# Vision transformer block on one core: the low parts of one weight row move from VectorE to GpSimd, and the layer-norm statistics start right behind the second block of low parts

## What is computed

```python
h = _L0_tok_ref(x, ln_gamma, ln_beta, W, b)     # shifted patches, layer norm over 3840 values, einsum to 192
h = concatenate([cls_tok, h], axis=1)
h = h + _L0_attn_ref(_layernorm(h), w_q, b_q, w_k, b_k, w_v, b_v, w_o, b_o, bias_table)   # 12 heads of 16
h = h + _L0_ffn_ref(_layernorm(h), router_w, w_gate, w_up, w_down, ws_gate, ws_up, ws_down, sg_w, sg_b)
return h                                        # (16, 37, 192)
```

## Time and profile before

| | |
|---|---|
| median of 3 runs | 155.25 us (154.12 to 157.67) |
| the profiled execution | 153.76 us, of which span 151.7 us |
| PE busy | 136.1 us, 90% of the span |
| DVE busy | 105.2 us, 69% |
| ACT busy | 85.6 us, 56% |
| POOL busy | 50.8 us, 33% |
| mean granted TensorE clock | 0.989 of full speed |

### The profile page before, as it was taken

How to read it: one execution, slowest core, us unless ns; L and a number is a source line. 1 busy time by engine, 2 the same in 40 slices (tenths; PEclk the granted TensorE clock), 3 DMA queues, 4 the chain that set the end, 5 groups by cost and what they waited for, 6 DMA issues and landing times.

```text
span 151.7 us, 3991 instructions
## 1 busy us (share of the span) xinstructions
PE 136.1 (90%) x1554; PEld 107.3 (71%) x1554; DVE 105.2 (69%) x268; ACT 85.6 (56%) x206; POOL 50.8 (33%) x72
## 2 busy tenths in 40 slices
PE   7769999999969879995869999998999999999991
PEld 2228678875558768975538868886887888888890
DVE  6499997899978768895275999857946423423553
ACT  0578779632687794663258877556455344444330
POOL 8038002400000000000003334388478477477330
PEclk9999999999999999998799999999999999999999
DMA  4999992095002323006993000146980000000003
GB/s 122 394 370 389 289 289 64 7 322 244 0 4 68 64 68 64 4 4 209 393 413 127 4 0 0 64 135 231 295 250 3 0 0 4 0 0 4 2 0 120
DMA packets 10580, 19.05 MB, mean 126 GB/s; under 512 B 2886, under 2 KB 6290, under 8 KB 10562
## 3 DMA queue, kind: packets, MB, share of 16 engines
q1 hardware_dynamic: 10218, 18.48, 37.2%
q10 hardware_dynamic: 344, 0.32, 0.8%
HBM read 17.84 MB, written 0.96 MB: 124 GB/s over the span
## 4 chain that ended last, share of the span: by engine, by line
PE 49%; DVE 27%; ACT 10%; issue 5%; DMA 4%; POOL 2%; DVEq 0%; SPq 0%; POOLq 0%; ACTq 0%
PE PS L810 22%; PE PS L840 12%; DVE we L1247 6%; DMA slab<-in_w_inner_dram 4%; DVE xhl L1225 2%; DVE bst L1356 2%; PE PS L622 2%; PE PS L670 2%; DVE piece L1296 2%; DVE vhl L1561 2%; PE PS L700 1%; POOL vhl L1182 1%; ACT piece L961 1%; DVE h L1390 1%; DVE xs L1440 1%
## 5 line engine op out<-in xcount | busy, mean ns | idle before, releaser
L1191 POOL TENSOR_TENSOR kq<-vhl,kq 128x296 f16<-128x296 f32 x35 | 28.2, 805 | 71.2 <-ACT kq L1098 71.1
L1561 DVE SCALAR_TENSOR_TENSOR vhl<-PS,vhl 128x296 f32<-128x296 f32 x36 | 16.8, 465 | 21.2 <-POOL vhl L1182 13.7
L1091 ACT ACTIVATE vhl<-PS 128x296 f32<-128x296 f32 x36 | 14.9, 415 | 25.3 <-PE PS L810 25.2
L1098 ACT ACTIVATE kq<-vhl 128x296 f16<-128x296 f32 x36 | 16.0, 445 | 4.2 <-DVE vhl L1561 4.2
L1182 POOL TENSOR_TENSOR vhl<-vhl,xs 128x296 f32<-128x296 f32 x14 | 12.5, 892 | 6.8 <-issue 6.1
L810 PE MATMUL PS<-XAh,piece 128*128 128x296 f16 x48 | 9.5, 289 | 1.6 <-ACT XAh L978 0.7
L810 PE MATMUL PS<-XAh,slab 128*128 128x296 f16 x48 | 10.0, 289 | 0.7 <-DVE vhl L1561 0.7
L1247 DVE SCALAR_TENSOR_TENSOR we<-slab,gbs,we 128x192 f32<-128x192 f32 x24 | 9.0, 444 | 2.0 <-ACT we L899 2.0
L810 PE MATMUL PS<-XAh,xsq 128*128 128x296 f16 x48 | 10.0, 289 | 0.0
L502 PE MATMUL PS<-whl,xhl 128*128 128x192 f16 (+1 forms) x40 | 9.9, 247 | 0.0
L504 PE MATMUL PS<-whl,xhl 128*128 128x192 f16 (+1 forms) x40 | 9.9, 246 | 0.0
(11 more groups left out here) (242 smaller groups left out, 367.3 us busy)
## 6 DMA issues: line engine op xcount, KB each, us to landing
slab<-in_w_inner_dram SPq DMA_DIRECT2D x3, 960.0 KB, 9.4
xs<-gate_rows_dram SPq DMA_DIRECT2D x8, 296.0 KB, 6.3
xs<-in_x_inner_dram SPq DMA_DIRECT2D x3, 592.0 KB, 10.3
stage<-in_f_a_dram SPq DMA_DIRECT2D x2, 768.0 KB, 4.7
stage<-in_f_b_dram SPq DMA_DIRECT2D x2, 768.0 KB, 6.3
stage<-gate_rows_dram SPq DMA_DIRECT2D x8, 148.0 KB, 6.0
stage<-in_f_d_dram SPq DMA_DIRECT2D x2, 576.0 KB, 7.2
xhl<-in_f_a_dram SPq DMA_DIRECT2D x1, 768.0 KB, 8.8
```

Source lines behind the costliest of these rows:

```text
L1091: A(silu[:, i % 2, :], PS[:, 3 + 2 * (i % 2), 0:HALF], ACT.Silu, scale=1.0 / XW).then_inc(S["a_silu"], 1)
L1098: A(ah[:, f % ABUF, half * HALF:(half + 1) * HALF], hf[:, i % 3, :], ACT.Copy).then_inc(S["a_ah"], 1)
L1191: G.tensor_tensor(al[:, f % ABUF, cols], hf[:, i % 3, :], ah[:, f % ABUF, cols], ALU.subtract).then_inc(S["g_al"], 1)
L1561: V.scalar_tensor_tensor(out=hf[:, i % 3, :], in0=PS[:, 4 + 2 * (i % 2), 0:HALF], scalar=SH / XW, in1=src[:, i % 2, :], op0=ALU.mult, op1= ...
```

## The change

Three things are changed.

1. The low parts of piece 2 (row 96 of `WC`) are made on GpSimd. It first scales the row of `awst` into a new buffer `brow` (1 x 1161), and then subtracts the high parts in four instructions (128, 128, 256 and 393 columns), each of which waits for the one before. It signals `g_br`, for which TensorE waits in the places where it waited for the last `v_awl`. VectorE loses five instructions in `queries_keys_low(2)` and one in `values_low(2)`.
2. `column_total()` stands ahead of `last_patches(2)` on TensorE.
3. VectorE waits for `csum` inside `centred(0)`, and `centred(1)` stands behind `rsqrt(0)`.

```diff
--- before.py
+++ after.py
@@ -162,6 +162,7 @@
         awst = sb("awst", [P, 3, AW])
         WAh, WAl, WB = (sb(n, [P, PW], F16) for n in ("WAh", "WAl", "WB"))
         WC = sb("WC", [CROWS, PW], F16)
+        brow = sb("brow", [CROWS, AW])
         kodd = sb("kodd", [P, 1])
         keven = sb("keven", [P, 1])
 
@@ -232,7 +233,7 @@
                    a_fw a_silu a_ah
                    v_one v_ind v_pad v_aw0 v_kk v_xl v_fold v_ring v_wl v_mr v_awl v_stat v_c v_h v_hn v_lo  v_kb v_sg v_max v_sub
                    v_cn v_rd v_lg v_dif v_gate v_gx v_fw v_hf v_acc v_fin v_al v_bn
-                   g_tab g_mk g_one g_vz g_v1 g_rows g_sg g_al""".split()
+                   g_tab g_mk g_one g_vz g_v1 g_rows g_br g_sg g_al""".split()
         S = {n: sem(n) for n in names}
 
         def bank(b, rows=P):
@@ -568,8 +569,8 @@
             for t in (0, 1):
                 last_patches(t)
             statistics()
+            column_total()
             last_patches(2)
-            column_total()
             for t in (0, 1, 2):
                 bias(t)
             for t in (3, 4):
@@ -615,7 +616,10 @@
                     pe.wait_ge(S["v_c"], TILES)
                 if f == 0 and i in (0, 2, 4):
                     pe.wait_ge(S["a_aw"], 3 + 3 * (i // 2))
+                if f == 0 and i in (0, 2):
                     pe.wait_ge(S["v_awl"], 5 + 5 * (i // 2))
+                if f == 0 and i == 4:
+                    pe.wait_ge(S["g_br"], 4)
                 c0 = ((KA, KB), (QA, QB))[q][g]
                 if f in (0, 4):
                     tokens_ready(0, half, i)
@@ -639,7 +643,8 @@
             def values(i):
 
                 pe.wait_ge(S["a_aw"], 12)
-                pe.wait_ge(S["v_awl"], 18)
+                pe.wait_ge(S["v_awl"], 12)
+                pe.wait_ge(S["g_br"], 5)
                 if i >= 2:
                     pe.wait_ge(S["a_hi"], 4)
                     pe.wait_ge(S["v_lo"], 4)
@@ -1169,6 +1174,23 @@
             G.memset(CA[:, N:NPAD], 0.0)
             G.memset(CC[:, N:NPAD], 0.0).then_inc(S["g_rows"], 1)
 
+            pool.wait_ge(S["g_rows"], 2)
+            pool.wait_ge(d_aw[2], 48)
+            G.tensor_scalar(brow[96:CROWS, :], awst[96:CROWS, 2, :], SW, None, ALU.mult).then_inc(S["g_br"], 1)
+            pool.wait_ge(S["a_aw"], 9)
+            low = slice(96, CROWS)
+            heads = brow[low, 0:VC].rearrange("p (q c) -> p q c", q=2)
+            for g in (0, 1):
+                pool.wait_ge(S["g_br"], g + 1)
+                h = heads[:, :, g * P:(g + 1) * P].rearrange("p q (r c d) -> p c q r d", r=LANES, c=2)[:, 0]
+                G.tensor_tensor(lane_cols(WC[low], g), h, lane_cols(WC[low], g), ALU.subtract).then_inc(S["g_br"], 1)
+            pool.wait_ge(S["g_br"], 3)
+            G.tensor_tensor(third_packed(WC[low, QB:VP]), heads[:, :, 2 * P:3 * P], third_packed(WC[low, QB:VP]),
+                            ALU.subtract).then_inc(S["g_br"], 1)
+            pool.wait_ge(S["g_br"], 4)
+            pool.wait_ge(S["a_aw"], 12)
+            G.tensor_tensor(WC[low, VP:PW], brow[low, VC:AW], WC[low, VP:PW], ALU.subtract).then_inc(S["g_br"], 1)
+
 
             def gated(i):
 
@@ -1264,7 +1286,7 @@
                 cols = sum_half(half)
                 V.tensor_copy(sumrows[rows, cols], PS[rows, half, 0:cols.stop - cols.start]).then_inc(S["v_mr"], 1)
 
-            low_of = ((WAl, WAh, slice(0, P)), (WB, WB, slice(64, P)), (WC, WC, slice(96, CROWS)))
+            low_of = ((WAl, WAh, slice(0, P)), (WB, WB, slice(64, P)))
 
             def queries_keys_low(k):
 
@@ -1296,7 +1318,7 @@
                 V.scalar_tensor_tensor(out=W[r0:P, part], in0=st[r0:P, part], scalar=SW, in1=hi[r0:P, part],
                                        op0=ALU.mult, op1=ALU.subtract).then_inc(S["v_fw"], 1)
 
-            for k in range(3):
+            for k in range(2):
                 queries_keys_low(k)
 
             stat = [0]
@@ -1326,6 +1348,8 @@
             nmean, nsq = small[:, 6, :], small[:, 7, :]
 
             def centred(t):
+                if t == 0:
+                    dve.wait_ge(S["a_cs"], 2)
                 dve.wait_ge(S["p_main"], (2, 2, 3, 5, 5)[t])
                 V.scalar_tensor_tensor(out=t1[:, t, :], in0=csum[:, :], scalar=small[:, 6, t:t + 1],
                                        in1=patch_out(t), op0=ALU.mult,
@@ -1339,10 +1363,9 @@
             step(V.scalar_tensor_tensor(out=small[:, 3, :], in0=sums[:, 1], scalar=1.0 / (32 * PATCH_DIM), in1=nsq,
                                         op0=ALU.mult, op1=ALU.add))
             step(V.tensor_scalar(small[:, 0, :], small[:, 3, :], 0.0, EPS, ALU.max, ALU.add))
-            dve.wait_ge(S["a_cs"], 2)
-            for t in (0, 1):
-                centred(t)
+            centred(0)
             rsqrt(0, 1.0 / (SPIX * SPW))
+            centred(1)
 
             bn = [0]
 
@@ -1415,7 +1438,6 @@
             normed(0, (3, 4))
             keys_third(1)
             values_low(1)
-            values_low(2)
             low_parts(0, (1, 2, 0), 1)
 
             def differences(u):
```

## The result

| | before | changed |
|---|---|---|
| median | 154.69 us (4 runs, 153.63 to 157.67) | 157.62 us (4 runs, 156.34 to 158.82) |
| ratio, 95% interval | | 1.027 (1.020 to 1.035) |

The change makes the kernel slower by 2.7%, and 0.5% faster was forecast. That it is slower is clear of the interval; whether by more than 2% is not. The profiled execution took 158.82 us and has a span of 156.8 us; it is the longest of the four, because the clock fell for long in it, so its span is not used for differences, only its rows.

The account below looks back on a forecast made before the run. It took 28 to 44 us as bound by VectorE's chain of small steps, not TensorE. Gain 0.89 us less hold-ups 0.15 us gives 0.74 us; 155.25 - 0.74 = 154.5 us, range 152.9 to 156.7 us.

Parts of the forecast that it names:

- What GpSimd costs VectorE: Step on VectorE's small steps, 28.4 to 34 us: hold-ups by GpSimd cost 0.15 us, between 0 and 2.0 us.
- The bound of 0.40 us for one hold-up: Worst VectorE wait seen: a `we` instruction of 805 ns, median 410 ns, begun beside a GpSimd subtraction of 0.63 us.
- the five steps: VectorE instructions reading two SBUF operands, 28.4 to 34 us: one statistics step, three in `rsqrt(0)`, one in `values_low(0)`; 0.40 us each at most.
- hold-ups eat the gain: slower: Rival at the small steps from 29.1 us: GpSimd delays VectorE's two-SBUF-operand instructions, up to 2.0 us, giving 156.4 us; chance 0.15.
- the clock falls otherwise: Rival on TensorE's clock, dip at 70 to 74 us: one dip less or more, 1.4 us, 153.1 or 155.9 us; chance 0.08.
- the room of 0.9 us behind the statistics matmuls: Statistics matmuls end at 29.04 us, VectorE reads them at 29.97 us: room 0.93 us, gain 0.89 us.
- the low parts of `WC` as what filled it: Five VectorE instructions on `WC`, 28.96 to 29.94 us, stand ahead of the first statistics step; without them it starts at 29.08 us.
- the new order at zero: Putting `centred(1)` behind `rsqrt(0)` was costed at 0, between 0 and a loss of 0.1 us.
- the transposes that don't move: TensorE's transposes stay at 37.27 us behind 22 warming matmuls, 0.1 us earlier at most.
- the first low part of the tokens at 38.78 us: VectorE's low parts of the normed tokens start 0.89 us earlier, 0.16 us behind ScalarE's first high part.
- the scores at 43.0 us: TensorE's first scores, at 43.89 us before, start at about 43.0 us.
- the gain that reaches the end: Behind the scores no row shows a wait with its own clock, so the 0.89 us shift carries through at full size.

## Why the prediction was wrong

**The step that failed** is "What GpSimd costs VectorE". It put all hold-ups at 0.15 us, between 0 and 5 x 0.40 us. They were 2.60 us in the trace. Two things in it were wrong. The bound of 0.40 us for one hold-up came from a GpSimd instruction of 0.63 us; the hold lasted until about the end of that instruction, so with one of 3.17 us it can be up to 3 us. The scale of the bound should have been the length of GpSimd's instruction, not the excess seen beside a short one. And the condition was too narrow: only the subtractions went into the 0.15 us, while the scaling held the second step for 1.92 us, and steps with one operand in SBUF were not counted, while one was held for 0.20 us in the changed kernel and one for 1.8 us when the second step read PSUM. A smaller slip hid behind it: of the five steps, the one in `values_low(0)` comes only at 36.51 us, after GpSimd has ended. (What it calls subtractions of the kernel before are additions of two operands in the program, which changes no number.)

**The rival "hold-ups eat the gain: slower"** had the mechanism, the place and the point of decision (0.89 us), with a chance of 0.15. Its price was mis-sized for the same reason, 2.0 us at most where 2.60 us were measured, and its 156.4 us lie below the median. Its argument against itself, that operands of 5 columns make it harmless, was of no weight: steps of 128 x 5 and of 1 x 64 values waited for 1.9 and 2.2 us.

**The clock.** The rival "the clock falls otherwise" priced a fall at 1.4 us (1.6 us was measured) but treated falls as single events of a chance of 0.08. In fact the kernel before has one or more in 30 of 35 runs, and the changed kernel in all of its eight. The medians are 2.9 and 2.3 us apart, of which 1.66 us are the hold-up. That the change itself brings more or longer falls, and so the other 0.6 to 1.3 us, is not shown. In its first four runs the clock was 0.970 on average; in the second four it was 0.978, and 0.979 in the 25 runs of the kernel before beside them. At an equal clock of 0.978 four runs of the changed kernel took 156.34 to 157.71 us and 21 of the kernel before 154.50 to 155.36 us, 1.9 us between their medians, which is little more than the hold-up. One page had led to the view that the clock was full but for two slices; the spread of the runs from 154.12 to 157.67 us already told otherwise.

**Right, each shown by a run:** the room of 0.9 us behind the statistics matmuls; the low parts of `WC` as what filled it; the new order at zero; the transposes that don't move; the first low part of the tokens at 38.78 us, barely behind ScalarE; the scores at 43.0 us; the gain that reaches the end (0.7 to 0.8 us of the 0.89 us). GpSimd was never waited for: its last instruction ends at 34.19 us, 33.9 us was forecast, and the scaling took 3.17 us for 2.7 us. VectorE was to be less busy by 1.6 us and is busier by 1.0 us, which is the 2.60 us of waits: they stand in the records as busy time. The range (152.9 to 156.7 us) was too narrow upwards by 0.9 us, for it held only one of the two effects at a time, and the chance of 0.05 for slower by over 2% rested on the same.

## What to carry to other kernels

Work moved to an idle GpSimd is not free for VectorE, even where the two share no data: for each of its instructions ask how long it is and which VectorE instructions start in that time, and bound the wait by the length of GpSimd's instruction. In a trace such a wait looks like a VectorE instruction many times its usual length that ends together with one of GpSimd's. If VectorE is on the path there with small steps on SBUF, keep GpSimd still, give the long part to ScalarE, or lay GpSimd's work beside VectorE's reads of PSUM. And look at the spread of the runs before judging an effect under 2%: here the clock moved single runs in steps of 1.6 us, and matmuls that keep TensorE busy through its waits made differences of 0.7 us readable.

## What the runs showed of the hardware that was not expected

- One GpSimd scaling of one partition by 1161 columns (3.17 us) held a VectorE instruction on 128 x 5 values for 1.9 us and one on 1 x 64 values for about 2.2 us, both with two operands in SBUF. It held a maximum and addition on one 32-bit operand in SBUF for 1.8 us. On record the 128 x 5 step with two operands ended 0.24 us ahead of the scaling, and the one with one operand 0.03 us behind it (31.18 and 31.15 us). Instructions with an operand in PSUM ran at their usual 0.16 us beside it, and at 0.41 us beside the subtractions.
- A RECIPROCAL with its one operand in SBUF wasn't held: 0.16 us at 35.06 us, beside a subtraction that ran from 34.79 to 35.67 us. What sets it apart from the other steps with one operand no run shows.
- The same scaling in nine instructions took 5.34 us, 0.59 us for 129 columns, and made no step beside it longer by more than 0.13 us.
- GpSimd's clears held nothing in the kernel before. The four low parts of `WB` take 0.64 us beside clears, as the four of `WC` do with GpSimd idle:

```profile
27.59 0.64 DVE L1275 SCALAR_TENSOR_TENSOR WB<-awst,WB 64x64 f16<-64x64 f32 x4
...
27.44 0.63 POOL L1167 MEMSET wring<- 64x640 f16 x1
```

- The waiting goes the other way too. GpSimd's instruction on two operands of 37 columns, 1.31 us from 11.12 us, began while the first of these VectorE instructions with two operands in SBUF ran, and ended 0.14 us behind it:

```profile
10.85 1.44 DVE L1225 SCALAR_TENSOR_TENSOR xhl<-xs,xhl 128x1184 f16<-128x1184 f32 x1
12.21 0.64 DVE L1234 SCALAR_TENSOR_TENSOR whl<-we,whl 128x384 f16<-128x384 f32 x1
12.77 0.52 DVE L1247 SCALAR_TENSOR_TENSOR we<-slab,gbs,we 128x192 f32<-128x192 f32 x1
```

- GpSimd's scaling of 222 columns, 0.97 us from 12.52 us, began during the second of them, and the `we` instruction behind it took only 0.52 us for its usual 0.41 us. Why that scaling held up so little stays open: VectorE was at work first there, and the scaling differs in partitions, in its repeated input and in its 16-bit output.
